# Four GNN layers on one core: one q tile of each head turned by VectorE and by DMAs through DRAM, and the regroup of the attention outputs issued by GpSimd

## The reference

```python
qkv = (x @ w_qkv).reshape(b, n, 3, H, hd).transpose(2, 0, 3, 1, 4)
attn = jnp.einsum('bhnd,bhmd->bhnm', q, k) * scale
attn = jnp.where(attn_mask[None, None] == 0, -jnp.inf, attn)
attn = jax.nn.softmax(attn, axis=-1)
o = jnp.einsum('bhnm,bhmd->bhnd', attn, v).transpose(0, 2, 1, 3).reshape(b, n, d)
o = o @ w_proj + b_proj
...
return o + ln
```

## Time and profile before

| | |
|---|---|
| median of 3 runs | 2798.15 us (2797.14 to 2798.94) |
| the profiled execution | 2797.58 us, span 2795.7 us |
| granted TensorE clock | 0.997 of full speed |
| PE, DVE, ACT, POOL busy | 2762.8, 2250.6, 2062.7, 1126.7 us |
| transposes of T on PE (L885) | 8192 |
| copies into PT, ACT and DVE | 1376 of 597 ns, 672 of 690 ns |

### The profile page before, as it was taken

The page is one execution under the profiler, slowest core; times in us unless marked ns, Lnnn a source line. Parts: engine busy times, 40 slices in busy tenths (PEclk is TensorE's granted clock), DMA queues, the critical chain, the costliest instruction groups (busy, mean ns, idle before and its releaser), DMA issues.

```text
span 2795.7 us, 60283 instructions
## 1 busy us (share of the span) xinstructions
PE 2762.8 (99%) x23520; PEld 2219.0 (79%) x23520; DVE 2250.6 (81%) x4144; ACT 2062.7 (74%) x3711; POOL 1126.7 (40%) x1088
## 2 busy tenths in 40 slices
PE   9999999999999999999999999999999999999998
PEld 7888888687778787878787877787778777778776
DVE  6776766888888888888888888888888888888876
ACT  3000001988888889898889888888888888888886
POOL 2222321225556464637373747242424242415131
PEclk9999999999999999999999999999999999999999
DMA  3001002434343434343434363434344343434333
GB/s 132 31 31 61 31 31 61 103 75 111 78 108 90 108 87 104 88 111 83 116 80 111 87 163 94 103 82 110 83 100 99 90 103 87 110 81 114 85 92 84
DMA packets 170601, 251.32 MB, mean 90 GB/s; under 512 B 33328, under 2 KB 135216, under 8 KB 170320
## 3 DMA queue, kind: packets, MB, share of 16 engines
q1 hardware_dynamic: 169120, 243.14, 34.7%
q0 software_dynamic: 1200, 4.33, 0.5%
HBM read 70.65 MB, written 25.69 MB: 34 GB/s over the span
## 4 chain that ended last, share of the span: by engine, by line
PE 70%; POOL 5%; issue 2%; ACT 2%; DVE 2%; DMA 1%; SPq 0%; POOLq 0%; ACTq 0%; DVEq 0%
PE t_ring_ps L885 28%; PE t_ot_ps L913 15%; PE t_s_ps L872 14%; PE t_ring_ps L855 4%; PE t_ring_ps L856 4%; PE t_ring_ps L857 4%; POOL t_xe L1397 2%; ACT t_T L1074 1%; PE t_ring_ps L945 1%; ACT PT L1080 1%; POOL t_oT_lo L1472 1%; POOL t_ot L1461 1%; DVE t_T L1164 1%; DMA t_R_ot<-inverse_row_sums 1%; DMA inverse_row_sums<-t_rT 1%
## 5 line engine op out<-in xcount | busy, mean ns | idle before, releaser
L1164 DVE CUSTOM_DVE_ANT_0 t_T<-t_s_ps,mask 128x1024 f32<-128x1024 f32 x1024 | 1233.4, 1215 | 114.4 <-PE t_s_ps L872 107.7
L1074 ACT ACTIVATE t_T<-t_T,t_low 128x1024 f32<-128x1024 f32 x1024 | 1170.8, 1150 | 23.5 <-DVE t_low L1164 20.2
L885 PEld LDWEIGHTS t_ring_ps<-ident,t_T 128*128 128x128 f32 x8192 | 933.7, 141 | 213.3 <-issue 72.2
L885 PE MATMUL t_ring_ps<-ident,t_T 128*128 128x128 f32 x8192 | 1088.8, 274 | 7.7 <-ACT t_T L1074 2.8
L1080 ACT ACTIVATE PT<-t_ring_ps 128x512 f32<-128x512 f32 x1376 | 757.3, 597 | 230.0 <-PE t_ring_ps L885 220.5
L872 PE MATMUL t_s_ps<-t_k,t_q 128*128 128x512 f32 x2048 | 727.4, 436 | 1.6 <-DVE t_low L1164 1.5
L1249 DVE COPY PT<-t_ring_ps 128x512 f32<-128x512 f32 x672 | 460.9, 690 | 191.0 <-PE t_ring_ps L885 185.0
L913 PE MATMUL t_ot_ps<-PT,shared 128*32 128x256 f32 x8192 | 494.9, 382 | 0.2 <-ACT PT L1080 0.2
L913 PEld LDWEIGHTS t_ot_ps<-PT,shared 128*32 128x32 f32 x8192 | 240.0, 109 | 217.0 <-ACT PT L1080 45.0
L273 ACT ACTIVATE g_yT_hi<-g_ps 128x512 fp32r<-128x512 f32 x64 | 38.3, 599 | 379.3 <-PE g_ps L205 379.3
L872 PEld LDWEIGHTS t_s_ps<-t_k,t_q 128*128 128x128 f32 x2048 | 309.2, 191 | 5.6 <-DVE t_low L1164 5.0
(11 more groups left out here) (186 smaller groups left out, 3743.3 us busy)
## 6 DMA issues: line engine op xcount, KB each, us to landing
t_q<-t_st_hi SPq DMA_DIRECT2D x256, 128.0 KB, 2.3
t_q<-t_st_lo SPq DMA_DIRECT2D x256, 128.0 KB, 2.4
t_k<-t_st_hi SPq DMA_DIRECT2D x256, 128.0 KB, 2.4
t_k<-t_st_lo SPq DMA_DIRECT2D x256, 128.0 KB, 2.4
t_R_ot<-inverse_row_sums SPq DMA_DIRECT2D x256, 64.0 KB, 2.0
t_oT_raw<-t_ot SPq DMA_DIRECT2D x512, 32.0 KB, 1.9
shared<-x_after_graph_layers SPq DMA_DIRECT2D x8, 1024.0 KB, 6.3
t_xe<-x_after_graph_layers SPq DMA_DIRECT2D x32, 256.0 KB, 3.2
```

Source lines behind the costliest of these rows:

```text
L885: last = nc.tensor.transpose(banks[b][:, i * P:(i + 1) * P], T[u % RING][:, kt * P:(kt + 1) * P], ident[:])
L1074: nc.scalar.activation(T[u % RING][:], T[u % RING][:], ACT.Exp, bias=low[:, u % RING:u % RING + 1], scale=-1.0, accum_out=rsum[:, u:u + 1] ...
L1164: nc.vector.tensor_tensor_reduce(out=T[u % RING][:], in0=s_ps[u % 2][:], in1=mask[:, qt, :], scale=1.0, scalar=3.4e38, op0=ALU.add, op1=AL ...
```

## The change

One q tile of each head (`FLIPS = (0,)`, units with u % 8 == 0) is no longer transposed by TensorE. VectorE turns its `T` in blocks of 32 x 32 into `turned_T`; SP writes that to DRAM (`turned_rows`) and reads it back in four DMAs, one for each 32 partitions, straight into `PT`. A block transposition puts other keys on a partition than a full one, so the four chunks of 32 that make up a key tile are taken across: for the q tiles 0 and 1, which one matmul reads together, PT is kept "in chunks", and their values matmuls read runs of 32 elements. The flipped unit uses no bank of the ring and no `copy_pt`.

GpSimd issues the regroup, right after each `scale_ot`, and the last scaling of the job before with its regroup stands ahead of `move_v`. `spread_rows` is cut into `write_rows` and `read_rows`, with the reads into PT between. `copy_ot` stands earlier on ScalarE. The values stand ahead of the group's first block on TensorE. The tables of blocks and of who copies what are new: `BOTH_ON_ACT` has 28 units in place of 22. Layer 3's weights are kept in DRAM and loaded over layer 2's in jobs 7 and 8; this makes room in SBUF.

```diff
-EARLY = [(1, ("norm", 3)), (11, ("out", 0)), (14, ("out", 1)), (27, ("out", 2)), (30, ("out", 3))]
+EARLY = [(1, ("norm", 3)), (11, ("out", 0)), (15, ("out", 1)), (19, ("out", 2)), (26, ("out", 3))]
...
+FLIPS = (0,)
...
+            def move_turned(job, h, i):
+
+                n = HEADS * job + h
+                sp.wait_ge(T_turned[i], n + 1)
+                if n:
+
+                    sp.wait_ge(turned_in[i], 64 * n)
+                sp.dma_start(turned_rows[i].rearrange("c p f -> p c f"),
+                             turned_T[i][:].rearrange("p (c f) -> p c f", c=NT)).then_inc(turned_out[i], 16)
+
+            def place_turned(job, h, i):
+
+                n, qt = HEADS * job + h, FLIPS[i]
+                sp.wait_ge(turned_out[i], 16 * (n + 1))
+                if n:
+
+                    sp.wait_ge(av_done, NT * (n - 1) + (HT if qt < HT else NT))
+                for j in range(4):
+                    rows = slice(j * HD, (j + 1) * HD)
+                    sp.dma_start(PT[rows, qt, :, :] if h % 2 == 0 else PT[rows, :, qt, :],
+                                 turned_rows[i][2 * j:2 * j + 2].rearrange("h (g k) f -> k (h g) f", g=4)).then_inc(turned_in[i], 16)
...
             def transposes(job, u, half):
 
+                if u % NT in FLIPS:
+                    return
...
+                if kt == 0:
+
+                    for i in range(len(FLIPS)):
+                        pe.wait_ge(turned_in[i], 64 * (NT * job + u // NT))
                 for j in range(HT):
-                    probs = PT[:, 2 * j:2 * j + 2, kt, :] if h % 2 == 0 else PT[:, kt, 2 * j:2 * j + 2, :]
+                    pair = slice(2 * j, 2 * j + 2)
+                    if in_chunks(2 * j):
+                        chunks, cols = slice(kt // HT * HT, (kt // HT + 1) * HT), slice(kt % HT * HD, (kt % HT + 1) * HD)
+                        probs = PT[:, pair, chunks, cols] if h % 2 == 0 else                             PT[:, chunks, pair, cols].rearrange("p g t q -> p t g q")
+                    else:
+                        probs = PT[:, pair, kt, :] if h % 2 == 0 else PT[:, kt, pair, :]
...
+            def turn_T(job, u):
+
+                if u % NT not in FLIPS:
+                    return
+                i, n = FLIPS.index(u % NT), HEADS * job + u // NT
+                dve.wait_ge(p_done, UNITS * job + u + 1)
+                if n:
+
+                    dve.wait_ge(turned_out[i], 16 * n)
+                nc.vector.transpose(turned_T[i][:].rearrange("p (j c q) -> p c j q", j=4, c=NT),
+                                    T[u % RING][:].rearrange("p (c j q) -> p c j q", j=4, c=NT)).then_inc(T_turned[i], 1)
...
+            def regroup(job, pr):
+
+                pair = 4 * job + pr
+                pool.wait_ge(scaled, pair + 1)
...
+                for j in range(4):
+                    for hh in range(2):
+                        h = 2 * pr + hh
+                        pool.dma_start(oT_raw[h % GH * HD:(h % GH + 1) * HD, h // GH, 2 * j * P:2 * (j + 1) * P],
+                                     ot_sb[j * HD:(j + 1) * HD, 2 * hh * P:2 * (hh + 1) * P]).then_inc(regroup_in[j], 16)
...
             def body(job, layer, before, after):
+                if before is not None:
+                    scale_ot(job - 1, 3)
+                    regroup(job - 1, 3)
                 move_v(job)
                 if before is not None:
-                    scale_ot(job - 1, 3)
...
-                    for p in range(XE):
-                        bias_xe(job - 1, before, p)
+                    bias_xe(job - 1, before, 0)
                     turn(job - 1, 0)
+                    bias_xe(job - 1, before, 1)
+                    bias_xe(job - 1, before, 2)
                     turn(job - 1, 1)
```

More of the change, by code:

```diff
@@ L758, in spread_rows @@
                                  row_scratch[:, 2 * j * P:2 * (j + 1) * P].partition_broadcast(HD)).then_inc(rows_in, 16)
[L760 to L777, removed]
             def body(job, layer, before, after):
+                move_head(job, 0)
                 if before is not None:
-                    for p in range(XE):
-                        load_xe(job - 1, before, p)
-                    spread_rows(job - 1, 3, key_of(job, ("norm", 3)))
-                    regroup(job - 1, 3, (0,))
+                    write_rows(job - 1, 3, key_of(job, ("norm", 3)))
+                place_head(job, 0)
+                if before is not None:
+                    read_rows(job - 1, 3)
                 load_head(job, 2, UNITS * job + 8, None)
-                if before is not None:
-                    regroup(job - 1, 3, (1,))
+                move_head(job, 1)
                 if after is not None:
@@ L803, in body @@
                     load_xe(job - 1, before, 3)
+                if job == 0:
+                    save_weights(2)
+                    save_weights(3)
                 load_head(job, 4, UNITS * job + 24, (job, 1))
+                if layer != after and after is not None:
+                    load_weights(slice(0, 3 * D))
+                move_head(job, 3)
+                place_head(job, 3)
                 if before is not None:
@@ L814, in body @@
                 load_head(job, 7, UNITS * job + 48, None)
+                move_head(job, 6)
+                write_rows(job, 2, key_of(job, ("norm", 2)))
+                place_head(job, 6)
+                read_rows(job, 2)
                 if before is not None:
                     store(job - 1, before, 3, key_of(job, ("out", 3)))
[L817 removed]
+                if before is not None and before != layer:
+                    load_weights(slice(3 * D, 4 * D))
                 if before is not None:
@@ L821, in body @@
                 if after is not None:
+                    for p in range(XE):
+                        load_xe(job, layer, p)
                     load_head(job + 1, 0, UNITS * job + 56, (job, 0))
-                regroup(job, 2)
+                move_head(job, 7)
+                place_head(job, 7)
                 if after is not None:
@@ L963, in body @@
                 table = blocks_of(before is None, after is not None)
-                if layer != after and after is not None:
-                    pe.wait_ge(w_split, 4)
                 def block_of(u):
@@ L1114, in body @@
                     exp(job, u + 1)
+                    if u % (2 * NT) == NT - GROUP and (u >= NT or before is not None):
+                        copy_ot(UNITS * job + u + GROUP - NT)
                     exp(job, u + 2)
@@ L1515, in body @@
                 scale_ot(job, 1)
+                regroup(job, 1)
                 if before == 0:
```

177 lines of the change are left out of this document (117 added, 60 removed).

## The result

The changed kernel takes 2765.5 us (median of four runs, 2763.3 to 2768.2) against 2797.8 for the kernel before in the same session: ratio 0.9884, 95% interval 0.9869 to 0.9900, 32 us saved. The forecast was 2735 in 2697 to 2795. The direction holds and the range holds the time, but half of the 63 us forecast is missing. The profiled execution has a span of 2762.0 us (2763.8 as timed).

A forecast was written before the change was run, and what follows sets the result against it. The prediction took TensorE's own stream as the bound, with no slack in the chain feeding ("out", 0). It summed 2797.6 - 105.0 + 29 + 13 = 2734.6, so 2735 us, in a range of 2697 to 2795.

The forecast's parts named there:

- (b): SP's queue: waits for writes make R_ot or head 7's tile 2 to 4 us late each job; 2765 to 2795; chance 0.17.
- (c): Flipped groups: VectorE becomes the bound, slower, with a transposition of 2.4 us; 2874, or 2836 with heavier groups; chance 0.13.
- TensorE sets the time: Attention jobs: TensorE's own stream is the bound, busy 143.0 of 143.3 us a job.
- 105 us for the transposes less 13 for VectorE: Flipped tiles: TensorE saves 6.56 us a job, 105.0 in all; VectorE's short groups cost 0.8 a job, 13 us.
- reading runs of 32: Values matmuls of the first q tile pair: cost taken as zero; 3 us a head if one column group were twice as slow.
- "Expected cost 0" for the transfers: Flipped tile's write to DRAM and reads into PT: 8.5 us from the transposition, hidden; cost 0, bound 3 us a job.
- The 1 to 4 us of slack given to head 7's tile: Head 7's tile: SP has the next job's load_head in front of it, leaving only 1 to 4 us of slack.
- The wait at ("out", 0), 29 us: Output projection: eight GpSimd issues lengthen its chain to 9.9 us; TensorE waits 2.4 us, not 0.46, in 15 jobs.
- "The second regroup ... Hidden": GpSimd: the second regroup puts 4.4 us ahead of norm; 17 us of work fit in 27 us, so no cost.
- (a): GpSimd's chain to ("out", 0): all the gain arrives, TensorE waits no more than now; 2693 to 2706 us; chance 0.2.

The follow-up runs named there:

- experiment 1: On the changed kernel, GpSimd's turn for ("out", 0) is put ahead of move_v and the first bias addition: 2735.55 us, ratio 0.9779.
- experiment 2: On the changed kernel, GpSimd adds the bias for ("out", 3) before scaling and regrouping the first pair of heads: 2751.26 us, ratio 0.9832.
- experiment 9: On experiment 5, no q tile is flipped (FLIPS empty), so TensorE transposes all of them again: 2794.77 us, ratio 0.9988.
- experiment 5: On the changed kernel, the edits of experiment 1 and experiment 2 together: 2723.49 us, ratio 0.9735.
- experiment 6: On experiment 5, SP issues layer 3's last two weight saves (job 0) and first 1.5 MB load (job 7) behind head 3's flipped tile: 2716.53 us, ratio 0.9711.
- experiment 11: On experiment 6, the eight loads of layer 3's mask (4 MB) are left out, VectorE's mask passes kept without effect: 2709.29 us, ratio 0.9684.
- experiment 7: On experiment 5, VectorE does each block transposition twice, one after the other: 2830.64 us, ratio 1.0116.
- experiment 3: On the changed kernel, SP issues the whole regroup again, at the places of the kernel before: 2819.44 us, ratio 1.0073.
- experiment 8: On the changed kernel, SP issues R_ot's four loads before the flipped tile's four into PT at a job's start: 2750.37 us, ratio 0.9830.

## Why the prediction was right, and what it missed

**The number.** The forecast was 31 us low. The flip gave 21 us less than reckoned and a wait that was priced at nothing cost 14; the other terms nearly cancel. That 2765.5 lies in the range is luck, or the width that was left for rivals (b) and (c); it lies a hair inside the forecast's own upper end of 2766, which had been worked out from slower issues, not from either of these.

**TensorE sets the time.** Right. Each us taken off its waits came back as a us or more: 22.5 us of waits as 30 (experiment 1), 12.7 as 14 (experiment 2).

**105 us for the transposes less 13 for VectorE.** The transposes fell to 7168, the transposition takes 1.23 us (some 1.16 from start to start, where 1.15 was taken), reading runs of 32 costs nothing (379 ns at the median, as in the earlier trace rows), and the first group takes 7.16 us where 7.33 was reckoned. But with GpSimd's waits out of the way the flip gives 71 us, not 92. Job by job, experiment 9 less experiment 5:

| jobs | no flip | flip | gain |
|---|---|---|---|
| 1 | 143.2 | 137.2 | 6.0 |
| 0 | 141.3 | 141.2 | 0.1 |
| 7 | 143.5 | 141.9 | 1.6 |
| 8 | 146.6 | 151.5 | -4.9 |

Twelve jobs, 1 to 6 and 9 to 14, keep 5.7 to 6.0 of 6.56: 0.7 is lost on the mean where 0.8 was charged, 0.3 of it in the first group, VectorE's as foretold. Jobs 0, 7 and 8 give -3 us together, where 3 x 5.8 = 17 was forecast. The last job gives 3.4 us (155.1 less 151.7 to the end); its group from unit 48 even grows, 7.7 to 8.2 us.

No transposition is slowed by GpSimd, though 62 of the 128 run beside one of its passes, 85 if its DMA issues are counted (line 1340: min/median/max in ns):

```profile
L1340 DVE STREAM_TRANSPOSE t_turned_T<-t_T x128: 1174/1240/1244, 488.9 to 2726.2; 128x1024 f32<-128x1024 f32 x128
```

The Trainium skill, "SBUF — State Buffer", section "SBUF: two separate sides", has the lock between GpSimd and VectorE for VectorE's operations in a two-port mode or with two inputs in SBUF; by these rows it doesn't reach the transposition. The estimate of 1.2 us from the Trainium skill, "VectorE: DVE Perf Modes", section "The three transpose paths", agrees with the row's 1240 ns.

**"Expected cost 0" for the transfers** is the first step that failed. It looked at a usual job. Three aren't usual: job 0 saves the weights, job 7 loads them, and at the end of job 7 GpSimd loads 4 MB of mask. A tile that goes through DRAM crosses the DMA engines twice, and SP waits for the first crossing; where 3 us each was reckoned, the median is 3.4 for the write and 2.7 for a read, but the slowest of either takes 10.6 us in the changed kernel. Experiments 6 and 11 show it for jobs 7 and 8 by moving or taking away these transfers: job 7 has all of it back (138.2 us in experiment 6 where it took 141.9). Job 0 has not: in experiment 11 TensorE still waits 2.9 us there for head 0's tile, and no run tells why. The 1 to 4 us of slack given to head 7's tile held in the other jobs (1.2 to 2.4 us in jobs 1 to 6 and 8 to 14 of the changed kernel, from the last landing to the values).

**The wait at ("out", 0), 29 us.** Right in its mechanism, and too large: experiment 1 gives 30 back, of which some 0.3 to 0.46 us a job was there before, so 23 to 25 were added. In job 11 the chain runs from 12.09 to 21.83 us (9.7, forecast 9.9) and TensorE is there at 20.3: that is 1.5 us, not 2.4, because the chain starts 0.9 us sooner, and its row has 1.39 of it as idle. Eight jobs idle 1.1 to 1.4 us. Where R_ot lands later TensorE idles up to 2.65 us, and in two jobs the wait costs 4 us because the clock falls (last section), which the prediction didn't have; without that the term would have been further off.

**"The second regroup ... Hidden"** is the second step that failed, and the plainer one: 14 us. The prediction looked for what the issues put ahead of norm. It didn't look at the addition for ("out", 3), which stands between them and norm, and whose consumer the change moved from unit 30 to unit 26, 9 us earlier. The issues made it 4 us later from the one side, the new table took the cover from the other.

**Rivals.** (a) fell with the 23 us of waits at L922. (c) fell at 1.23 us. Its price was 101 to 139 us above the forecast (2836 to 2874 less 2735); at 2.5 us a tile experiment 7 measures 107, near the lower end. (b) gave the right time, 2765, by the wrong road. It had SP late by 2 to 4 us in every job; measured, TensorE waits for a tile in three (0, 7 and 8), and the bias makes up most of the rest. Experiment 3 shows how near (b) was: with the regroup left on SP it holds in nearly every job and costs 54 us.

**The sum, as it stands now:** 2797.8 - 3 (the new order with edits 1 and 2 but no flip, experiment 9) - 71 (the flip) + 30 (the turn) + 14 (the bias) = 2768, 2 us above what was measured, within the runs' spread. Since the last three terms come from runs of these kernels, the sum shows only that they add.

What stays open: what takes the rest of a usual job's loss (0.2 us each in the group from unit 16, 10.4 us without the flip and 9.8 with it, and in the one from unit 56, 7.4 and 6.7; others gain a little more than 0.82); what holds the last job's groups; what makes head 0's tile late in job 0; and whether another order of transfers gives back job 8's loss, which wasn't tried.

## What to carry to other kernels

Issuing a DMA is work of the engine that issues it: go through everything queued behind the issues up to the next wait, and ask of each when its consumer wants it after the change, not before. Here two moved calls, the turn and the bias, were worth 42 us, more than the change itself had brought. A detour through DRAM is priced where the transfers are densest (weights, masks, the seams between layers), not in the usual period.

## What the hardware showed beyond that

TensorE's granted clock can fall behind a wait, and the wait then costs more than its length. In job 8 of the changed kernel TensorE idles 5.5 us from 1610.65 on, until the tile is there. Two windows of that job, with the columns of the earlier trace rows:

```profile
1614.00:1615.00 1.00, 0.00 (x0) 0.00 (x0) 0.97 (x2) 0.00 (x0) 0.00 (x0) 0.93 1.05 260
1616.00:1621.00 5.00, 4.87 (x36) 2.57 (x37) 1.22 (x2) 0.65 (x2) 0.00 (x0) 0.50 1.04 265
```

The clock goes to 0.50 (1.2 of 2.4 GHz) some 1.3 us before the wait ends and stays there while TensorE works again, until about 1621.7. The 32 values behind the wait take 3.64 us:

```profile
1616.13 3.64 PE L991 MATMUL t_ot_ps<-PT,shared 128*32 128x256 f32 x32 [5.48 <-DMA PT<-turned_rows]
```

In a usual group they take 1.93. This group is 15.8 us long and TensorE is busy 9.65 of it; in experiment 11, without the wait, 7.76 of 10.0: some 2 us on top of the wait. The third groups of the changed kernel show the same in small. Those of jobs 11 and 5:

```profile
2058.14:2067.72 9.58, 8.19 (x79) 6.26 (x78) 7.96 (x14) 6.75 (x14) 9.50 (x13) 1.00 0.86 247
```

```profile
1200.47:1212.69 12.22, 9.62 (x79) 7.68 (x78) 8.09 (x14) 6.75 (x14) 11.18 (x16) 0.86 0.96 248
```

In job 11 TensorE idles 1.39 us at ("out", 0) and its clock stays at 1.00; so it does in the twelve others with 1.14 to 2.46 us. In jobs 5 and 9, with 2.60 and 2.65 us, the group's clock is 0.86, TensorE is busy 9.6 us with the work of 8.2, and the wait costs 4 us. Behind the 3.76 us of experiment 3 the values take 2.88 us. Idle time alone may not decide it; what else does, these runs don't separate.

A small transfer's landing varies: one of R_ot's 64 KB lands 2.2 us after issue at the median, but the last in job 4 of experiment 8 took 3.9. The load of the DMA engines doesn't explain it: their share over the first 13 us of that job is 0.52, against 0.65 and 0.59 in jobs 3 and 11, where the same load took 2.0 and 2.5. And two neighbours in a queue needn't land in order: of the eight regroup transfers in job 11 of the changed kernel (32 KB each, 0.49 us apart) the fourth lands after the fifth.
